# Layer 1's gathers in a two-layer attention and expert kernel: four ranks added by DMA, four gathered plain and added on VectorE

## The reference, cut to what matters

```python
aff = xf @ centroids.T                               # 2048 x 64
_, idx = jax.lax.top_k(aff + expert_biases, 8)       # 8 experts for each token
w = jax.nn.sigmoid(jnp.take_along_axis(aff, idx, axis=1))
w = w / (jnp.sum(w, axis=-1, keepdims=True) + 1e-08)
h = jax.nn.silu(jnp.einsum('td,edf->etf', xf, W_up))
y = jnp.einsum('etf,efd->etd', h, W_down)
routed = jnp.einsum('etd,te->td', y, cw)             # cw holds w at idx
x = x + shared + routed
```

## Time and profile before

| | |
|---|---|
| time, median of 3 runs | 1048.6 us (1046.49 to 1048.81) |
| the profiled execution's own time | 1056.91 us |
| its span, from the first to the last instruction | 1055.0 us |
| busy PE, DVE, ACT, POOL | 840.2, 491.9, 383.2, 411.1 us |
| indirect DMAs with an add (line 1974) | 112, 173.8 us of POOL |
| plain ones of the same loop (line 1971) | 16, 15.3 us of POOL |

### The profile page before, as it was taken

One profiled execution on the slowest core, in us unless ns is written; L12 is line 12 of the kernel. 1 busy time (PEld: TensorE's weight loads), 2 busy tenths in 40 slices (PEclk: granted clock), 3 DMA queues, 4 the chain that ended last, 5 costly groups with the idle time before them and its releaser, 6 DMA issues.

```text
span 1055.0 us, 21664 instructions
## 1 busy us (share of the span) xinstructions
PE 840.2 (80%) x6226; PEld 725.7 (69%) x6226; DVE 491.9 (47%) x1691; ACT 383.2 (36%) x1374; POOL 411.1 (39%) x401
## 2 busy tenths in 40 slices
PE   5899999899999998899998998599989998900000
PEld 4788887699999976667766666488878987800000
DVE  3666665412211236787787865265444444400002
ACT  1222222311111156565655552156556655500000
POOL 3100000111111111566666556400213078888886
PEclk9899999799999999999999999799999999955555
DMA  8466777799999839722222225577889999965556
GB/s 249 160 238 244 254 269 269 260 299 329 323 328 331 289 94 292 246 88 92 89 90 86 89 81 170 176 222 240 254 265 277 279 268 290 275 103 73 70 85 124
DMA packets 179377, 217.90 MB, mean 207 GB/s; under 512 B 13904, under 2 KB 164688, under 8 KB 179280
## 3 DMA queue, kind: packets, MB, share of 16 engines
q1 hardware_dynamic: 123408, 143.31, 42.0%
q0 software_dynamic: 25344, 44.06, 18.0%
q10 hardware_dynamic: 30528, 29.37, 8.2%
HBM read 126.64 MB, written 90.05 MB: 205 GB/s over the span
## 4 chain that ended last, share of the span: by engine, by line
PE 57%; issue 16%; DVE 10%; DMA 5%; ACT 4%; POOL 4%; POOLq 2%; DVEq 1%; SPq 1%; another core or an unknown queue 0%; ACTq 0%
PE PS L786 11%; PE PS L1034 5%; PE PS L1041 5%; PE PS L796 5%; DMA Q<-queue 4%; PE PS L654 3%; PE PS L672 3%; PE PS L865 3%; PE PS L1022 3%; PE PS L875 3%; ACT R L1238 2%; PE PS L912 2%; POOL Q L1974 2%; PE PS L632 2%; DVE nmax L1576 2%
## 5 line engine op out<-in xcount | busy, mean ns | idle before, releaser
L1974 POOL DMA_INDIRECT Q<-routed,slot x112 | 173.8, 1552 | 63.9 <-issue 32.7
L1923 POOL DMA_INDIRECT queue<-Q,slot x128 | 125.7, 982 | 86.4 <-DVE nmax L1576 53.6
L1034 PEld LDWEIGHTS PS<-Q 128*128 128x128 f32 x768 | 116.8, 195 | 24.4 <-issue 9.3
L1238 ACT ACTIVATE R<-PS,nmax 128x154 f32<-128x154 f32 x256 | 108.3, 547 | 56.5 <-DVE nmax L1576 46.1
L1034 PE MATMUL PS<-Q 128*128 128x128 f32 x768 | 120.5, 280 | 9.9 <-DVE Q L1763 5.2
L786 PEld LDWEIGHTS PS<-R 128*128 128x128 f32 x992 | 115.2, 192 | 4.3 <-issue 2.6
L786 PE MATMUL PS<-R 128*128 128x128 f32 x992 | 116.2, 275 | 1.3 <-ACT R L1200 1.1
L1763 DVE COPY Q<-R 128x256 f32 x192 | 58.2, 304 | 126.1 <-PE PS L1041 86.4
L1041 PE MATMUL PS<-R,Q 128*128 x384 | 116.3, 386 | 0.0
L1307 ACT ACTIVATE Q<-PS 128x128 f32<-128x128 f32 x192 | 53.5, 279 | 99.9 <-PE PS L1041 77.7
L1022 PE MATMUL PS<-ident,Q 128*128 128x128 f32 x384 | 76.9, 283 | 9.8 <-DMA Q<-queue 9.1
(11 more groups left out here) (281 smaller groups left out, 1588.3 us busy)
## 6 DMA issues: line engine op xcount, KB each, us to landing
R<-in_gate_up SPq DMA_DIRECT2D x31, 1024.0 KB
Q<-queue SPq DMA_DIRECT2D x192, 160.0 KB
routed<-pads SPq DMA_DIRECT2D x16, 1536.0 KB, 6.9
routed<-Q ACTq DMA_DIRECT2D x96, 256.0 KB
R<-in_down SPq DMA_DIRECT2D x31, 512.0 KB
queue<-pads SPq DMA_DIRECT2D x16, 640.0 KB, 3.3
R<-in_W_up SPq DMA_DIRECT2D x16, 512.0 KB
R<-in_W_down SPq DMA_DIRECT2D x8, 1024.0 KB
```

The source lines that it names most:

```text
L1034: pe.matmul(up1_bank(j), w_now[:, j % BEHIND, c, :], x1T[:, j % BEHIND, c, :], start=(c == 0), stop=(c == KC - 1))
L1238: i = act.activation(prob[:, g % 2].rearrange("p (k h) -> p h k", h=HG)[:, h, :], src, ACT.Exp, bias=nmax2[:, g % 2, h:h + 1], accum_out=d ...
L1923: pool.indirect_dma_start(out=queue1, out_offset=bass.IndirectOffsetOnAxis(ap=slot1[:, t * TOP1 + k:t * TOP1 + k + 1], axis=0), in_=pay[:, ...
L1974: pool.indirect_dma_start(out=acc[:, t, :], out_offset=None, in_=routed1, in_offset=rows, compute_op=ALU.add).then_inc(S(f"acc_in{t}"), 16)
```

## The change

The order of the gathers stays: ranks are now counted upwards, `r` = 0 being the row that is made first, which the code gets by storing `BIG` minus the row number. Ranks 0 to 3 (`ADDED` = 4) go as before: `r` = 0 is written plain to `acc[:, t]`, 1 to 3 are added into it by the DMA. Ranks 4 to 7 are plain gathers into memory of their own, `sum_part(r - 4, t % 2)`. That memory is the front of `R`: 8192 floats from 0 (even tiles) and 8192 from `NUP` (odd tiles), where the weights of experts 0 to 31 lie. So the gathers of ranks 4 to 7 must not start before the last tile with rows is done, and their `need1` is raised to that tile's pair; the tiles behind it now name expert 63 instead of 0. VectorE adds what the DMA added before: ranks 5 and 6 onto rank 4 with four `tensor_tensor` of 2048 columns (`sum_rank`), and then `acc`, the sum of ranks 4 to 6, and rank 7 into `X` with three `scalar_tensor_tensor` of 256 columns on each tile where there was one. The waits on tiles' gathers keep one semaphore for each tile.

```diff
@@ the needs: expert loop, TensorE and VectorE @@
                 pe.matmul(bank(2)[:, 0:E1], ones1[0:E1, :], begin_diag[0:E1, :], start=True, stop=True).then_inc(S("begin_ps"), 1)
+                pe.wait_ge(S("end_rows"), nth("end_rows", 1))
+                pe.matmul(bank(2)[0:1, 3 * P:4 * P], end_col[0:E1, :], all_tiles[0:E1, :], start=True, stop=True).then_inc(S("end_row_ps"), 1)
...
-                dve.tensor_scalar(begin_col[:, :], first, float(P), None, ALU.add).then_inc(S("begin_col"), 1)
+                dve.tensor_scalar(begin_col[:, :], first, float(P) + BIG, None, ALU.add).then_inc(S("begin_col"), 1)
...
+                dve.memset(all_tiles, 0.0).then_inc(S("all_zero"), 1)
+                step("all_zero")
+                dve.memset(all_tiles[0:E1, ADDED * NT:], 1.0).then_inc(S("all_tiles"), 1)
+                dve.tensor_scalar(end_col[0:E1, :], ntiles, float(P), None, ALU.mult).then_inc(S("end_rows"), 1)
...
-                dve.tensor_scalar(need1[:, :], bank(2)[0:1, 2 * P:3 * P], float(PAIR * P - 1), None, ALU.add).then_inc(S("need_up1"), 1)
+                dve.tensor_scalar(need_row[0:1, :], bank(2)[0:1, 2 * P:3 * P], -1.0, BIG, ALU.mult, ALU.add).then_inc(S("need_row1"), 1)
+                step("need_row1")
+                dve.tensor_tensor(need_row[0:1, :], need_row[0:1, :], bank(2)[0:1, 3 * P:4 * P], ALU.max).then_inc(S("need_max1"), 1)
+                step("need_max1")
+                dve.tensor_scalar(need1[:, :], need_row[0:1, :], float(PAIR * P - 1), None, ALU.add).then_inc(S("need_up1"), 1)
@@ the end, VectorE @@
+            def sum_rank(r, odd):
+                for t in range(odd, NT, 2):
+                    dve.wait_ge(S(f"acc_in{t}"), nth(f"acc_in{t}", 16 * (r + 1)))
+                if r > ADDED + 1:
+                    dve.wait_ge(S("summed"), 2 * (r - ADDED - 2) + odd + 1)
+                dve.tensor_tensor(sum_part(0, odd), sum_part(0, odd), sum_part(r - ADDED, odd), ALU.add).then_inc(S("summed"), 1)
+
+            def into_x(r, t, name):
+                dve.scalar_tensor_tensor(X[:, t, :], gathered(r, t), rstd_all[:, t:t + 1], X[:, t, :], ALU.mult, ALU.add).then_inc(S(name), 1)
+
             for t in range(NT):
+                dve.wait_ge(S(f"acc_in{t}"), nth(f"acc_in{t}", 16 * ADDED))
+                into_x(0, t, "some_in")
+            for r in range(ADDED + 1, TOP1 - 1):
+                for odd in range(2):
+                    sum_rank(r, odd)
+            for t in range(NT):
+                dve.wait_ge(S("some_in"), t + 1)
+                dve.wait_ge(S("summed"), 2 * (TOP1 - ADDED - 3) + t % 2 + 1)
+                into_x(ADDED, t, "most_in")
+            for t in range(NT):
+                dve.wait_ge(S("most_in"), t + 1)
                 dve.wait_ge(S(f"acc_in{t}"), nth(f"acc_in{t}", 16 * TOP1))
-                dve.scalar_tensor_tensor(X[:, t, :], acc[:, t, :], rstd_all[:, t:t + 1], X[:, t, :], ALU.mult, ALU.add).then_inc(S("final"), 1)
+                into_x(TOP1 - 1, t, "final")
@@ the end, GpSimd @@
-            for k in reversed(range(TOP1)):
+            for r in range(TOP1):
                 for t in range(NT):
-                    i = t * TOP1 + k
+                    i = r * NT + t
                     need = pool.value_load(need1[0:1, i:i + 1], min_val=1, max_val=NX1 // PAIR)
                     pool.wait_ge(S("landed"), need)
                     pool.sem_inc(S("waited_pool"), 1)
+                    if r:
+                        pool.wait_ge(S(f"acc_in{t}"), nth(f"acc_in{t}", 16 * r))
                     rows = bass.IndirectOffsetOnAxis(ap=slot1[:, i:i + 1], axis=0)
-                    if k == TOP1 - 1:
-                        pool.indirect_dma_start(out=acc[:, t, :], out_offset=None, in_=routed1, in_offset=rows).then_inc(S(f"acc_in{t}"), 16)
+                    if 0 < r < ADDED:
+                        pool.indirect_dma_start(out=gathered(r, t), out_offset=None, in_=routed1, in_offset=rows,
+                                                compute_op=ALU.add).then_inc(S(f"acc_in{t}"), 16)
                     else:
-                        pool.wait_ge(S(f"acc_in{t}"), nth(f"acc_in{t}", 16 * (TOP1 - 1 - k)))
-                        pool.indirect_dma_start(out=acc[:, t, :], out_offset=None, in_=routed1, in_offset=rows,
-                                                compute_op=ALU.add).then_inc(S(f"acc_in{t}"), 16)
+                        pool.indirect_dma_start(out=gathered(r, t), out_offset=None, in_=routed1, in_offset=rows).then_inc(S(f"acc_in{t}"), 16)
```

More of the change, by code:

```diff
@@ L67, in build @@
     LAG = 14
+    ADDED = 4
+    BIG = float(1 << 15)
     LAND = 4
@@ L106, in build @@
                                "row1", "row_of1", "expert_of1")),
-            ("needs1_psum", ("begin_ps", "lastT_ps", "need_ps")),
-            ("needs1_steps", ("ones1", "begin_col", "begin_diag", "rows1", "last1")),
+            ("needs1_psum", ("begin_ps", "end_row_ps", "lastT_ps", "need_ps")),
+            ("needs1_steps", ("ones1", "begin_col", "begin_diag", "all_zero", "all_tiles", "end_rows", "rows1", "last1")),
             ("tile_rows_steps", ("moved1", "moved_sel1", "best_rows1")),
-            ("need_steps", ("need_up1", "need_of1")),
+            ("need_steps", ("need_row1", "need_max1", "need_up1", "need_of1")),
             ("route_psum", ("count_ps", "base_ps", "end_ps", "row_ps")),
@@ L313, in build @@
         x1T, w_now, h1T = q(BEHIND, KC, P), q(BEHIND, KC, F1), q(4, P)
-        tile_rows = q(NT, TOP1)
+        tile_rows = q(TOP1, NT)
         acc = q(NT, D)
-        active1, began1, row_at, ones1, begin_diag = (acc[:, i, 0:n] for i, n in enumerate((NX1, NX1, NX1, P, E1)))
+        active1, began1, row_at, ones1, begin_diag, all_tiles, end_col, need_row = (acc[:, i, 0:n] for i, n in enumerate((NX1, NX1, NX1, P, E1, P, 1, P)))
         PS = ctx.enter_context(nc.psum_tensor("PS", [P, 8, BANK], F32))
@@ L331, in x1_bank, with sum_part, gathered @@
             return bank((0, 1, 4)[j % BEHIND])[:, 0:D]
+        def sum_part(r, odd):
+            at = odd * NUP + r * (NT // 2) * D
+            return R[:, at:at + NT // 2 * D]
+        def gathered(r, t):
+            return acc[:, t, :] if r < ADDED else sum_part(r - ADDED, t % 2)[:, t // 2 * D:(t // 2 + 1) * D]
         def up1_bank(j):
@@ L1742, in _ @@
             dve.tensor_scalar(row_of[:, :], row_at[0:1, :], 0.0, None, ALU.max).then_inc(S("row_of1"), 1)
-            dve.tensor_copy(expert_of[:, :], bank(2)[0:1, 0:NX1]).then_inc(S("expert_of1"), 1)
+            dve.tensor_scalar(expert_of[:, :], bank(2)[0:1, 0:NX1], float(E1 - 1), None, ALU.add).then_inc(S("expert_of1"), 1)
             step("expert_of1")
@@ L1782, in begins @@
                 dve.memset(ones1, 1.0).then_inc(S("ones1"), 1)
-                dve.tensor_scalar(begin_col[:, :], first, float(P), None, ALU.add).then_inc(S("begin_col"), 1)
+                dve.tensor_scalar(begin_col[:, :], first, float(P) + BIG, None, ALU.add).then_inc(S("begin_col"), 1)
                 step("begin_col")
                 dve.tensor_scalar(begin_diag[0:E1, :], ident[0:E1, 0:E1], begin_col[:, :], None, ALU.mult).then_inc(S("begin_diag"), 1)
+                dve.memset(all_tiles, 0.0).then_inc(S("all_zero"), 1)
+                step("all_zero")
+                dve.memset(all_tiles[0:E1, ADDED * NT:], 1.0).then_inc(S("all_tiles"), 1)
+                dve.tensor_scalar(end_col[0:E1, :], ntiles, float(P), None, ALU.mult).then_inc(S("end_rows"), 1)
             def moved(t):
-                dve.tensor_tensor(row(weight, t), row(weight, t), bank(2)[:, 0:E1], ALU.subtract).then_inc(S("moved1"), 1)
+                dve.tensor_tensor(row(weight, t), bank(2)[:, 0:E1], row(weight, t), ALU.subtract).then_inc(S("moved1"), 1)
                 dve.wait_ge(S("moved1"), nth("moved1", t + 1))
@@ L1791, in moved @@
                 dve.wait_ge(S("moved_sel1"), nth("moved_sel1", t + 1))
-                dve.max(tile_rows[:, t], row(weight, t)).then_inc(S("best_rows1"), 1)
+                dve.max(tile_rows[:, :, t], row(weight, t)).then_inc(S("best_rows1"), 1)
             def rows():
                 dve.wait_ge(S("best_rows1"), nth("best_rows1", NT))
-                dve.tensor_scalar(slot1[:, :], tile_rows.rearrange("p t k -> p (t k)"), -1.0, None, ALU.add).then_inc(S("rows1"), 1)
+                dve.tensor_scalar(slot1[:, :], tile_rows.rearrange("p r t -> p (r t)"), -1.0, BIG - 1.0, ALU.mult, ALU.add).then_inc(S("rows1"), 1)
             def last():
                 step("lastT_ps")
-                dve.tensor_reduce(last_row[:, :], bank(2)[:, P:2 * P], X_AXIS, ALU.max).then_inc(S("last1"), 1)
+                dve.tensor_reduce(last_row[:, :], bank(2)[:, P:2 * P], X_AXIS, ALU.min).then_inc(S("last1"), 1)
             def needs():
                 step("need_ps")
-                dve.tensor_scalar(need1[:, :], bank(2)[0:1, 2 * P:3 * P], float(PAIR * P - 1), None, ALU.add).then_inc(S("need_up1"), 1)
```

(2 more changed lines are left out.)

4 lines of the change are left out of this document (2 added, 2 removed).

## The result

The changed kernel takes 1019.7 us (median of 4 runs, 1017.2 to 1021.0) against 1047.9 for the kernel before (median of 4, 1046.5 to 1048.8): a ratio of 0.973, 95% interval 0.971 to 0.975. It is 28.2 us faster. The forecast was 37.5 us faster, and 1019.7 lies above its range of 1006.5 to 1017. The rival that points there is the first one, "VectorE locks GpSimd out", which had got 9%; it named 1020 to 1028.

The account below looks back on a forecast made before the run. GpSimd's own time for each DMA was taken to bound the end; gathers -37.8, landing -1.1, stores +1.0 and needs +0.4 made -37.5 us, so 1048.6 became 1011.1 us. Ranges: 1007 to 1016 (80%), 1006.5 to 1017 (88% or a little less).

Parts of the forecast that it names:

- VectorE locks GpSimd out: Rival, 9%: VectorE's operations on two SBUF tensors hold GpSimd's gathers; sums cost 9.2 us, steps 7.7 more, 1020 to 1028.
- What bounds the kernel: From the 20th gather to the end: GpSimd's own time for each DMA, gathers following each other by 1.855 us.
- the new wait: Ranks 4 to 7 waiting for the last tile with rows: costs nothing, covered by 45 adds between 846.45 and 930.
- the worst case: All 192 tiles holding rows: last store landed at 928.43, 1.6 us before the 65th gather's turn at 930.03.
- The gathers: Last 64 gathers, plain instead of added: 1.255 us apart instead of 1.855, so the 128th starts 37.8 us earlier.
- The bound of 36.7: Lower bound of the gathers' gain in us, at the queue scatters' pace of 1.27 us per gather.
- VectorE's additions: Sums of 2.31 us and steps into X at the end: cost nothing as the likeliest, up to 3 us.
- Landing: Last gather's start to its rows being in: 2.86 us plain against 3.92 with an add, 1.1 us less.
- The stores: Stores of X beside the last gathers: 1 us against the change (0 to 3), landing growing from 1.8 to some 3.
- The needs: Extra small operations on VectorE and TensorE for the gathers' needs, ahead of the expert loop: 0.4 us (0 to 1).
- Sum: All terms together: -37.8 - 1.1 + 1.0 + 0.4 = -37.5 us, from 1048.6 to 1011.1 us.

Follow-up runs that it names:

- e6_phase: Kernel before plus single 0.48 us VectorE steps at five phases of a gather; three held gathers were over 1.42 to 1.43 us behind the step's end.
- e4_no_lock: Changed kernel with X in PSUM and 16 steps of 256 columns per rank instead of the four sums: median 1011.4 us, ratio 0.965.
- the two probes: Kernel before with five VectorE bursts beside GpSimd's adds, 212.5 us from the 20th gather to the end; and e6_phase.
- e2_pairs: Changed kernel with each tile's two last VectorE steps put together, both waiting for rank 7's gather: median 1015.1 us, ratio 0.969 to the kernel before.

## Why the prediction was wrong, point by point

- **What bounds the kernel, and the new wait**: right. POOL sets the pace from the 20th gather on and the 65th began with the usual 0.30 idle. The cover was 33 us, far thicker than the 1.6 us that the worst case left.
- **The gathers**: the price was right, 1.25 us from start to start wherever VectorE left them alone (923.14 to 963.27 is 32 steps of 1.254). But the 63 steps took 88.4 us for 79.1. (The bound of 36.7 should be 36.9: 63 steps of 1.27 are 80.0.)
- **VectorE's additions: the step that failed.** "Cost nothing as the likeliest" asked only whether VectorE would be late, and there it was near: the sums take 2.29 us, the last final step starts 0.10 us behind its gather's landing. What they do to GpSimd while they run was priced at nothing and left to a rival, at 9%, on the strength of the earlier trace rows; measured, they cost 10.9 us. The earlier trace rows show a step that begins behind a gather's start and can't hold it, which e6_phase made plain (and 14 of the last 16 adds have such a step, not each). The earlier trace rows show gathers beside copies of 0.3 us, which could hold one by 0.2 us at most; between 850 and 900 none began 0.05 to 0.17 us before a gather, which is where it would have held one. The one add that shows it, 1.59 us at 909.58, stood in the same trace outside both rows. The prediction itself wrote "none stands at a gather's start" and drew nothing from it. It also had the first 16 steps near 932 in VectorE's idle time, one at a time; 13 of them came in one run at 914.33, when VectorE was through with the expert loop and their rows had landed.
- **The rival was right in kind, and its price in part by luck.** Its 9.2 to 16.9 us hold the 10.9 measured, but it had each sum holding GpSimd for its length, 9.2 in all, and the sums cost 4.6, since each began before the gather that it held; the rest was the two long runs of steps, 1.4 and 4.6, and 0.4 in single steps. The Trainium skill, "SBUF — State Buffer", section "SBUF: two separate sides", has the mechanism, an exclusive lock on a port pair, and the runs agree that two inputs in SBUF and a copy from SBUF to SBUF take it and one input in PSUM doesn't. The traces show the hold and not the port. They differ from the same section in two points, and there the measurement decides: it says that whichever starts first has the pair for its whole instruction, where here a VectorE operation 0.18 us behind a gather ran its 2.29 us undisturbed; and its part "Who interferes with whom" tells of a probe in which a copy stalled a DMA and `tensor_tensor` didn't, where here a `tensor_tensor` lengthened an indirect DMA by 0.49 us.
- **Landing**: 1.1 us was taken, 0.46 came. The plain gathers' median is 2.8 us as forecast, but the last one took 3.46 (3.90 in e4_no_lock). It ran beside the stores, which may be why; no run separates it.
- **The stores**: 1.0 us was taken. From the last step's start to the end of the span are 4.1 us in both kernels, so nothing came behind the last step; the stores' median from issue to landing grew from 1.8 to 2.3 us where some 3 was forecast.
- **The needs**: 0.4 us was taken. The 20th gather starts at 838.10, and at 838.38 and 840.77 in the two probes with the needs of before. Nothing of that size shows; it wasn't measured by itself.
- **Sum**, from the 20th gather on: -28.5 for the 63 steps, +1.5 for the adds, nearly all beside the 13 steps at 914, -0.5 landing, 0 for the stores, -27.5 together. With the hold out of the way (e4_no_lock) the tail is 38.1 us shorter than before, where the forecast's own terms without the needs make 37.9. That this fits so well is partly luck: there the landing gave nothing for 1.1 and the stores took nothing for 1.0, and the two errors cancel.

## What to carry to other kernels

A free engine's work isn't free if it holds up the engine that sets the pace: beside GpSimd issuing indirect DMAs, give VectorE one SBUF input and one in PSUM, or short operations with gaps that don't lie over a gather's start. Rows that show two things side by side speak for no interference only if they overlap at the point where the resource is taken; ask at which phase they met. A rival that the rows can't exclude at that phase deserves more than the chance that is left over.

## What the runs showed of the hardware

- A gather of 128 rows of 1 KB takes GpSimd 0.95 us plain and 1.55 with an add. One that VectorE held was over 0.82 to 0.83 (plain) and 1.41 to 1.43 us (add) behind the end of the operation that held it; an operation that ended 0.12 us behind a gather's start held nothing.
- `tensor_tensor` and `scalar_tensor_tensor` with both inputs in SBUF hold it, and so does a float32 copy from SBUF to SBUF; with one input in PSUM they don't, at the same length (16 steps in 6.42 and 6.36 us).
- The earlier one wins. Copies that began 0.05 us or more before a gather held it; those that began within 0.04 us before waited themselves, for at most 0.07 us. For the steps of 0.48 us the border lay between 0.08 (the gather at 992.90 of the changed kernel was held) and 0.07 us (a step of e2_pairs waited). Runs of steps don't always keep to it, as the next point says.
- A run of short operations can hold a gather to its end. In the run of 16, one gather got in after a 0.2 us wait and the next waited 2.5 us; in the run of 21, one got in at once, one after 0.27 and the next waited 4.3. What decides whether a gather gets in between two steps stays open: the one at 991.65 and the one at 994.42 both began 0.02 us behind a step's start, and the first took 0.95 us and the second 5.24.
